# Dense steps three ahead of the edges' steps in one loop of a graph network, two ahead in another

## The reference

```
x = ln(x + sum over edges of sigmoid(z) * leaky(z))        # z from x[src], x[dst], edge_attr
x = ln(x + attention over edges, softmax by destination)   # first attention
h = relu(mean(x)[n] @ W1l.T + b1 + x @ W1r.T)              # first mean aggregation
x = ln(x + mean(h)[n] @ W2l.T + b2 + h @ W2r.T)            # second mean aggregation
Q, K = x @ qw, x @ kw                                      # second attention, 4 heads of 32
alpha = (Q[src] * K[dst]).sum / sqrt(32); a = softmax of alpha by destination
x = ln(x + (silu(ln(sum of a * Q[src]) * gamma + beta)) @ out_w + out_b)
```

## Time and profile before

| what | us |
|---|---|
| median of 3 runs (2856.81 to 2867.78) | 2858.34 |
| the profiled execution | 2850.63 |
| its span | 2848.9 |
| first mean aggregation, from the first running sum to the last mean | 1586.7 to 1862.2 |
| projection of the second attention, from the first load to the scan behind it | 2172.3 to 2489.7 |
| DVE busy in the span | 2281.0 (80%) |
| ACT busy in the span | 1733.1 (61%) |

### The profile page before, as it was taken

How to read it: one execution, slowest core, us unless ns; L and a number is a source line. 1 busy time by engine, 2 the same in 40 slices (tenths; PEclk the granted TensorE clock), 3 DMA queues, 4 the chain that set the end, 5 groups by cost and what they waited for, 6 DMA issues and landing times. The chain is left out here.

```text
span 2848.9 us, 51501 instructions
## 1 busy us (share of the span) xinstructions
PE 1850.4 (65%) x9787; PEld 1363.7 (48%) x9787; DVE 2281.0 (80%) x9061; ACT 1733.1 (61%) x4459; POOL 1692.5 (59%) x1605
## 2 busy tenths in 40 slices
PE   5666666566666625777776676667885666556673
PEld 4656555444544414454544343345664555524442
DVE  7887887999999927778888688857776999888882
ACT  3545454333332216777888688845665888868885
POOL 7777777266666664333332676647664766327675
PEclk8778777699888867898999899989997888867776
DMA  6777777445444437999999788868886888734441
GB/s 196 242 253 244 248 233 237 150 78 86 77 86 77 71 42 272 326 331 328 340 347 346 240 285 284 279 197 283 287 278 212 297 298 290 265 135 167 154 160 53
DMA packets 280135, 625.08 MB, mean 219 GB/s; under 512 B 51230, under 2 KB 84649, under 8 KB 280055
## 3 DMA queue, kind: packets, MB, share of 16 engines
q1 hardware_dynamic: 207543, 523.73, 53.0%
q0 software_dynamic: 72512, 100.52, 16.1%
HBM read 342.76 MB, written 285.23 MB: 220 GB/s over the span
## 5 line engine op out<-in xcount | busy, mean ns | idle before, releaser
L908 POOL DMA_INDIRECT sums<-gat_sums,dst_safe_i x196 | 186.0, 949 | 300.5 <-DVE pre L2158 250.9
L1381 ACT ACTIVATE node_out<-node_in,n_shift,n_root 128x128 f32<-128x128 f32 (+1 forms) x784 | 312.0, 483 | 45.6 <-DVE n_shift L1729 45.6
L1029 POOL DMA_INDIRECT out_dram<-node_x2t,out_index x196 | 208.3, 1063 | 156.7 <-ACT node_x2t L1616 96.7
L916 POOL DMA_INDIRECT src_rows<-x_table,row_i x200 | 200.0, 1000 | 105.3 <-issue 54.4
L916 POOL DMA_INDIRECT sums<-x_table,row_i x192 | 192.6, 1003 | 88.0 <-issue 50.9
L975 POOL DMA_INDIRECT gat_sums<-src_rows,add_idx x100 | 160.0, 1600 | 117.6 <-issue 25.7
L916 POOL DMA_INDIRECT own_rows<-in_x_dram,dst_safe_i x196 | 191.4, 976 | 59.8 <-issue 57.6
L975 POOL DMA_INDIRECT gat_sums<-sums,add_idx x96 | 152.8, 1592 | 91.3 <-issue 29.6
L1390 ACT ACTIVATE t_a<-ps 128x512 f32<-128x512 f32 (+1 forms) x198 | 115.9, 585 | 144.9 <-PE ps L1074 144.2
L1390 ACT ACTIVATE t_b<-ps 128x512 f32<-128x512 f32 (+1 forms) x198 | 116.3, 587 | 108.9 <-PE ps L1074 108.9
L1074 PE MATMUL ps<-ident,msg 128*128 128x128 f32 x590 | 102.4, 300 | 105.0 <-DVE msg L2215 53.9
(11 more groups left out here) (436 smaller groups left out, 6799.3 us busy)
## 6 DMA issues: line engine op xcount, KB each, us to landing
own_rows<-x_table SPq DMA_DIRECT2D x245, 256.0 KB
node_in<-in_x_dram SPq DMA_DIRECT2D x96, 512.0 KB
x_table<-node_out SPq DMA_DIRECT2D x84, 512.0 KB
x_table<-new_rows SPq DMA_DIRECT2D x147, 256.0 KB
gat_sums<-node_x2t SPq DMA_DIRECT2D x49, 528.0 KB, 4.3
acc_dump<-acc SPq DMA_DIRECT2D x98, 264.0 KB
node_sums<-gat_sums SPq DMA_DIRECT2D x48, 528.0 KB
h_table<-node_h SPq DMA_DIRECT2D x48, 512.0 KB
```

Source lines behind the costliest of these rows:

```text
L908: g_.indirect_dma_start(out=to[:, g.b, j, 0:width], out_offset=None, in_=tab, in_offset=bass.IndirectOffsetOnAxis(ap=indices(j), axis=0)). ...
L916: g_.indirect_dma_start(out=to4[g.q][:, j, 0:F], out_offset=None, in_=tab, in_offset=bass.IndirectOffsetOnAxis(ap=indices(j), axis=0)).the ...
L1029: g_.indirect_dma_start(out=out[:, :], out_offset=bass.IndirectOffsetOnAxis(ap=out_index[:, t:t + 1], axis=0), in_=wide_new[:, g.b, j, :], ...
L1381: last = sc.activation(to[0:pn, g.b, j, :], rows[0:pn, g.b, j, 0:F], ACT.Identity, bias=NORM[k][2][0:pn, g.b, j:j + 1], scale=root[0:pn, j ...
```

## The change

Only lags and one order are changed, for the same amount of work. In the first mean aggregation all the edges' stages of SP, ACT and DVE get a lag three turns longer, while the dense stages keep theirs. In the projection of the second attention all the edges' stages of SP, ACT and DVE get a lag two turns longer. There SP's list is also put in another order (the dense load stands ahead of the own rows' load), and the wait for the stored rows of the layer before moves from ahead of the loop into the first load of own rows. PE and POOL have only edges' stages in both places and are not touched. From the changed SP code on, line numbers of the kernel after are 5 higher.

```
-            pipeline(sp, DENSE_FULL, edges((0, load_own(L, L["tr_b"], x2_table, own_rows, L["own"])))
-                     + [packed(0, load_x3_nodes), packed(2, store_x3_nodes)] + edges((3, store)), per=4)
+            pipeline(sp, DENSE_FULL, edges((3, load_own(L, L["tr_b"], x2_table, own_rows, L["own"])))
+                     + [packed(0, load_x3_nodes), packed(2, store_x3_nodes)] + edges((6, store)), per=4)
...
-            wait_all(sp, flow["sage2"]["stored"])
-            sp.wait_ge(fix_out_sem, 16 * 3)
+            load_own_x3 = load_own_back(L, x3_table, own_rows)
+
+            def load_x3_own(g):
+                if g.first_use() and g.b == 0:
+                    wait_all(sp, flow["sage2"]["stored"])
+                    sp.wait_ge(fix_out_sem, 16 * 3)
+                load_own_x3(g)
...
-            pipeline(sp, DENSE_FULL, edges((0, load_own_back(L, x3_table, own_rows))) + [nodes(0, load_nodes(D, x3_table, SLOTS, "n_row"))]
-                     + edges((2, store_q)) + [nodes(2, store_nodes(D, out, 0))])
+            pipeline(sp, DENSE_FULL, [nodes(0, load_nodes(D, x3_table, SLOTS, "n_row"))] + edges((2, load_x3_own))
+                     + edges((4, store_q)) + [nodes(2, store_nodes(D, out, 0))])
...
-            pipeline(act, DENSE_FULL, [packed(1, x3_node_root)] + edges((2, h1_rows)) + [packed(1, x3_node_rows(0, DJ))]
-                     + edges((1, sage_relu), (0, sage_copies)), per=4)
+            pipeline(act, DENSE_FULL, [packed(1, x3_node_root)] + edges((5, h1_rows)) + [packed(1, x3_node_rows(0, DJ))]
+                     + edges((4, sage_relu), (3, sage_copies)), per=4)
...
-                     + edges((1, queries_keys_out), (0, att_copies)))
+                     + edges((3, queries_keys_out), (2, att_copies)))
...
-            firsts = [(0, mean_and_first(j)) for j in range(J)]
-            pipeline(dve, DENSE_FULL, edges((0, plain_sums)) + [packed(1, x3_node_shifts)] + edges((0, inverse_counts), *firsts)
+            firsts = [(3, mean_and_first(j)) for j in range(J)]
+            pipeline(dve, DENSE_FULL, edges((3, plain_sums)) + [packed(1, x3_node_shifts)] + edges((3, inverse_counts), *firsts)
...
-            spread = [(0, spread_row(L, i, own_rows, msg, "tr_b")) for i in range(J)]
+            spread = [(2, spread_row(L, i, own_rows, msg, "tr_b")) for i in range(J)]
...
-                     + edges(spread[2], (2, products), spread[3], (2, score_sums)) + [nodes(0, nodes_x3_more), nodes(0, nodes_x3_moments)])
+                     + edges(spread[2], (4, products), spread[3], (4, score_sums)) + [nodes(0, nodes_x3_more), nodes(0, nodes_x3_moments)])
```

## The result

The kernel after takes 3017.46 us (median of 4 runs, 3010.56 to 3022.03), the kernel before on the same chip 2857.57 (2855.07 to 2867.78): a ratio of 1.0579, 95% interval 1.0550 to 1.0607. The forecast was 2989, range 2945 to 3035. The profiled execution took 3022.03, span 3020.3.

A forecast was written before the change was run, and what follows sets the result against it. The prediction took DVE to bound both loops, with little air on ACT and the queues. It added +6 and +124.4 to the profiled 2850.63 for 2981, plus 7.7 for the median: 2989 us, range 2945 to 3035.

The forecast's parts named there:

- First mean aggregation, +6: That loop pays only at its ends, start 5.6, end +2.0 and -1.7, taken as +6 us; bounds 0 and +10.
- Second attention, start: Two dense steps fill DVE's wait; own rows stand behind dense load 2; first spread at 2181.9, against 2175.13 before.
- The ring: Second attention's turns: spread, shift, ACT's rows, dense load, own rows, landing, next spread; 9.0 us a turn against 6.27, 46 intervals.
- the landing of own rows behind that dense load, 4.65: Second attention: dense load's issue to next spread takes 4.65 us, from two earlier loads; added to 4.33 from spread to load.
- The sum: Whole kernel: +6 for the first mean aggregation, +124.4 for the second attention, +130.4 us in all.
- Same pace: Rival: second attention's loop keeps 6.27 us a turn because own rows still land in time; 2863 us, chance 0.04.
- faster: Rival: longer lag frees the second attention of small waits, turns fall to DVE's 5.7 us; 2837 us, chance 0.02.
- Longer ring: Rival: stores and gathers compete with own rows for the queues, 10.8 us a turn; 3072 us, chance 0.07.
- Partly hidden: Rival: own rows overtake most of the dense load, turns 6.3 to 8.0 us; 2863 to 2943, say 2915, chance 0.07.

The follow-up runs named there:

- e1: Kernel before with only the first mean aggregation's new lags, second attention as before: 2862.27 us, ratio 1.0028.
- e4: Kernel before with one edit, SP's dense load ahead of the own rows in the second attention, no lag changed: 3007.78 us, ratio 1.0574.
- e2: Kernel after, all its lags kept, but SP issues own rows ahead of the dense load in the second attention: 2860.77 us, ratio 1.0030.
- e3: Kernel after, dense load still first on SP, but own rows issued one turn sooner (lag 1 instead of 2): 2863.88 us, ratio 1.0039.
- e7: Kernel after, but ACT issues the second attention's own rows, listed right behind its normalised rows: 2864.69 us, ratio 1.0025.
- e9: Kernel after, but SP first waits for ACT's normalised rows, then issues own rows, then the dense load: 2932.49 us, ratio 1.0293.
- e10: Kernel after, but POOL's gathers in the second attention bring only 32 of 128 partitions: 3004.77 us, ratio 1.0528.
- e6: Kernel after, but the second attention's dense load brings 4 of 8 rows a partition, 256 KB instead of 512 KB: 2982.49 us, ratio 1.0455.
- e5: Kernel after, but the second attention's dense store carries one of 8 rows a partition, 64 KB instead of 512 KB: 3012.21 us, ratio 1.0547.

## Why the prediction was right, point by point

One row of the kernel before, beside those of the earlier trace rows, is needed for the landing below: the dense load that SP issued behind the first own rows.

```profile
1592.92 0.43 SPq L808 DMA_DIRECT2D node_in<-y_nodes  x1
```

- **First mean aggregation, +6.** Measured +6.2 in the stretch, +6.3 over all profiles; 2 to 14 us in the median, by e1. The repeated turns did not grow (5.59, before 5.62). The start came out to the tenth, which is luck: edge step 2 starts 28.1 behind the memset by the forecast and in this profile, 27.7 to 29.8 in the other eight with these lags.
- **Second attention, start.** From the closing row's copy to the first spread 12.0 was forecast (2181.9 - 2169.87), 12.2 measured. The two dense steps fill part of DVE's wait, and the third dense load holds the own rows, as said; DVE still idles 5.52 before the spread. That spread is at 2199.88 and not near 2188, mostly because the layers ahead of both loops and between them were slower in this profile (8.3 and 3.3, below).
- **The ring.** Shown, not only argued: it closes by SP's order alone (e4), opens by the order (e2), by the turn of issue (e3) or by an issue from ACT 3.1 ahead of SP's dense load (e7), and shortens when the bytes go behind (e9). The leg from spread to dense load was 4.35 for a forecast 4.33.
- **The mis-sized term: "the landing of own rows behind that dense load, 4.65".** It measured 5.27, so that a turn took 9.62 instead of 9.0. The 4.65 of the earlier trace rows was counted from the issue of the first of two loads. The second, the dense load, left 0.40 later (the row above), so from its own issue to its use it took 4.25. In the ring the second load is the own rows. They leave 0.67 behind the dense load and take 4.61 in the mean from their own issue to the spread. The same time is 4.68, 4.60 and 4.66 in three turns that stand ahead of the loop code (the first of them 2204.38 to 2209.06). Of the 0.62 that the term was short, about 0.27 is therefore the wider gap between SP's issues. The sum left it at the 0.40 of rows 6, though the earlier trace rows shows 0.67 between two issues of SP (2312.82 and 2313.49) and the prediction's own bounds count 0.6. The other 0.35 is a longer landing. The gathers are worth 0.3 in the ring (e10), yet gathers ran at the earlier trace rows too, so they don't account for it by themselves. Why the pair takes longer with the large load ahead than with the small one stays open.
- **The sum.** 46 turns by 0.58 more (9.58 from turn 2 to turn 48) are 26.5; start and end add 0.2 and 0.8 (18.9 from the last dense turn's spread to the scan, 18.1 forecast). 124.4 + 27.5 = 151.9, measured 151.8 (471.58 - 319.78). The profiled execution is longer by another 13.4 outside the two loops: 8.3 ahead of the first edit, 3.3 between the loops, 1.8 behind. These are not the change's: the memset ahead of the first edited instruction starts anywhere from 1580.7 to 1601.3 in these profiles. The medians differ by 160, the sum of the two stretches is 158.0.
- **The rivals.** "Same pace" and "faster" needed own rows to land within 1.9 (6.27 - 4.33) and 1.4 of the dense load's issue; 5.27 was measured. "Longer ring", from stores and gathers in competition, had the right sign and the wrong size (10.8 a turn): the dense store cost nothing, gathers 0.3; the store of Q was not tested. "Partly hidden" by overtaking did not occur.
- **The pages.** By "Anatomy of one DMA" of "DMA: Bandwidth & Descriptors" in the Trainium skill, 256 KB more cost 0.6 us (bytes at 436 GB/s) and the ring would have been 8.1, both estimates. The page gives that fit for transfers issued by the pool engine, which the prediction does not say, and these loads are issued by SP. e6 shows 0.8 for 256 KB, and the ring was 9.6. "Queues, rings and completion order" of the same page has descriptors consumed in ring order, and there the runs agree: own rows behind the dense load reach the spread 4.61 after their own issue in the mean, ahead of it, with the same bytes in all, 3.40 after (e9).

## What to carry to other kernels

When loads of two streams are issued by one in-order queue, ask of each load what waits of the same turn stand ahead of it and whether its data is used in the next turn: if the wait's releaser depends on that use, it is a ring, and its length, not any engine's work, is the turn. Close the circle on paper: add every leg, also the gap between two issues of the queue, and compare with the busiest engine's work per turn. The cure cost nothing that e2 and e3 could show: issue the load ahead of the wait, or one turn sooner.

## What the runs showed of the hardware that was not expected

- A DMA that ACT issues does not wait for ACT's earlier activations: it was issued 0.27 us after the first of eight started, 2.9 before the last ended (2407.51 + 2.79).
- SP's issues one right behind the other are 0.37 to 0.49 us apart in code ahead of the loop and 0.61 to 0.70 inside it. A turn of the ring takes 9.1 to 9.2 there and 9.62 in the loop; from spread to dense load it is 4.12 there and 4.35 in the loop.
- A large store 1.3 us behind a load in the same queue was free for it: taking away 448 KB a turn lowered the DMA rate from 194 to 149 GB/s and left the turn as it was (9.62 and 9.66, e5).
- TensorE's granted clock fell from 0.84 to 0.64 in the ring, a mix of its two levels (1.2 and 2.4 GHz), after PE had become idle in each turn (33.4 busy of 60 against 37.3). It cost nothing that the rows show: the legs of the circle, none of them PE's, add up to the whole turn.
